# State space stages: TensorE takes u*B first and the sum one unit behind, the gate follows the second scan, ScalarE draws items a unit later

## The chip, the cores and the metric

One core of a Trainium2 chip runs the whole program. The metric is the time of one execution on the device, in microseconds. Engines are named as the profile names them: TensorE (PE, its weight loads PEld), VectorE (DVE), ScalarE (ACT), GpSimd (POOL) and SyncE (SP), which issues DMAs.

## The reference, cut to what matters

The model is a decoder of two layers on an activation x of 4 batches x 512 positions x 256 channels, all in float32. Each layer is a state space block (Mamba), a cross attention and a feed forward part. The change touches the two state space blocks only. For one batch such a block computes:

```
xz = h @ in_proj_w.T;  x, z = split(xz)              # 512 inner channels each
xc = silu(conv4(x) + conv_b)                          # causal, 4 taps per channel
dt, Bm, Cm = split(xc @ x_proj_w.T)                   # 16 states in Bm and in Cm
dt = softplus(dt @ dt_proj_w.T + dt_proj_b)
h[t] = exp(dt[t] * A) * h[t-1] + (dt*xc)[t] * Bm[t]   # for each channel and each of 16 states
y[t] = sum over states of h[t] * Cm[t]
out = ((y + D * xc) * silu(z)) @ out_proj_w.T         # then added to the residual
```

The recurrence over t is the large part: 4 batches x 512 channels x 16 states x 512 positions, in each of the two blocks.

## The kernel before, in words

The program runs seven stages one after the other, with a barrier between neighbours. Stages "A" (from about 40 to 580 us of the span) and "B" (from about 1620 to 2160 us) are the state space blocks; both are written by the same functions, `mamba_pe`, `mamba_act`, `mamba_dve`, `mamba_pool` and `mamba_sp`.

**Units.** A stage has 128 units, 32 for each batch. A section of 8 units treats 128 inner channels (one partition each), a unit treats 2 of the 16 states at 512 positions, so a unit is a tile of 128 x 1024. Below, n is the number of a unit within its batch (0 to 31) and g within its section (0 to 7). For unit i:

- ScalarE makes the decays exp(dt*A) (`mamba_decay_act`, L656, two activations), in its slot i-2, so that it runs two units ahead. For g = 0, 1, 2, 4 and 6 they go to one of three PSUM places, used in turn (`i % RING_A`), and wait until unit i-3 has left that place; for g = 3, 5, 7 they go to one of two SBUF places.
- The input u*B with u = dt*xc: GpSimd multiplies it for g = 0, 1, 2, 4, 6 (L389); for g = 3, 5, 7 TensorE makes it with 8 matmuls against diagonal matrices (`mamba_input_pe`, L405), issued in its slot i-2.
- VectorE runs the scan over the positions (L850), then multiplies by the rows of C (L872) for g = 0, 1, 4, 6. For g = 2, 3, 5, 7 GpSimd multiplies (L430).
- TensorE sums: 8 transposing matmuls against the identity add the unit to y in PSUM (L543). For g = 0 this is preceded by D*xc (L538), which has to wait until the gate of the section before has read y.
- After the eighth sum of a section VectorE gates: yzT = y * silu(z) (`mamba_gate_dve`, L769). Before the change it is issued behind the scan of g = 0 of the next section and ahead of that unit's multiply.
- The products (`ch`) lie in a ring of four; whoever writes unit i waits for the sum of unit i-4.

**Items.** The dense work of the neighbouring batches is spread over the units as items: `h` (rows turned, L118), `in` and `z` (the halves of in_proj, L479 and L482), `conv` (L506), `xp` (L510), `dt` (L514), `bt` and `ut` (turns of B and of u), `yt` (the gated y turned back) and `out` (out_proj, L519). The tables `OWN`, `BEFORE` and `AHEAD` give for each n which item of this batch, of the one before and of the one after is due, and `mamba_items(i)` lists them for a unit. All items share one PSUM bank: an item on TensorE first waits until the item before has been drawn. ScalarE draws all items but `out`, which VectorE draws by adding it to x (L791) behind scan i+1, and `bt`, which VectorE's diagonals (L781) draw.

**Order of work.** Each engine has one hand written list and works it off in order. Before the change, TensorE's slot i is: the items of i, the input u*B of i+2, the sum of i. ScalarE's slot i is: the decays of i+2, `conv` items of slot i-1, the other items of slot i, then the occasional long ones: rows for the next batch (n = 4), silu of z (n = 5), a square root (n = 14), silu of the convolution (n = 22), the softplus (n = 26 to 28). Silu, square root and logarithm each need another activation table than the decays' exponential: a table load ahead and one behind.

Of the kernel before, what the change touches and what calls it, by code (L numbers as in the profile page):

```python
# [17 lines left out]
B, T, D = 4, 512, 256  # L18
# [151 lines left out]
UNITS = 8  # L170
PER = 4 * UNITS
RING_A = 3
RING_C = 4
# [5 lines left out]
def mamba_make(k, ctx, L, R, rms, rnd):  # L179
# [47 lines left out]
    if rms:  # L227
# [21 lines left out]

FIRST = [("h", 0), ("h", 1)] + [("in", i) for i in range(4)] + [("conv", 3), ("xp", 0)] + [("dt", i) for i in range(4)] + [("bt", 0)]  # L250
FIRST_BANKS = (0, 1, 2, 3, 4, 5, 6, 7, 0, 1, 3, 6, 2)
OWN = {1: ("z", 0), 2: ("z", 1), 3: ("z", 2), 4: ("z", 3), 13: ("yt", 0), 18: ("yt", 1), 25: ("yt", 2)}
BEFORE = {1: ("yt", 3), 6: ("out", 0), 8: ("out", 1), 10: ("out", 2), 12: ("out", 3)}
AHEAD = {5: ("h", 0), 6: ("h", 1), 7: ("in", 0), 9: ("in", 1), 11: ("in", 2), 14: ("in", 3),
         15: ("conv", 0), 17: ("conv", 1), 19: ("conv", 2), 21: ("conv", 3),
         23: ("xp", 0), 24: ("dt", 0), 25: ("dt", 1), 26: ("dt", 2), 27: ("dt", 3), 30: ("bt", 0)}


def mamba_items(i):

    b, s = i // PER, i % PER
    o = []
    if i == 0:
        o.append(("ut", 0, 0))
    if b and s in BEFORE:
        o.append((BEFORE[s][0], b - 1, BEFORE[s][1]))
    if s in OWN:
        o.append((OWN[s][0], b, OWN[s][1]))
    if s % UNITS == 6 and i // UNITS + 1 < 4 * B:
        n = i // UNITS + 1  # L270
        o.append(("ut", n // 4, n % 4))
    if b + 1 < B and s in AHEAD:
        o.append((AHEAD[s][0], b + 1, AHEAD[s][1]))
    return o


# [16 lines left out]
def from_pe(i):  # L293

    return i % UNITS in FROM_PE
# [15 lines left out]
def mamba_out(m, i):  # L311

    return m.met(MET[i]) if by_pool(i) else m.out(i - MET[i])
# [206 lines left out]
    p.then_inc(*m.full.up)  # L520


def mamba_pe(k, m, pe):
    for w, j in FIRST:
        mamba_item_pe(k, m, pe, w, 0, j)
    pe.wait_ge(*m.drawn(LEAD - 1))
    for i in range(PER * B):
        s, g = i // UNITS, i % UNITS
        for item in mamba_items(i):
            mamba_item_pe(k, m, pe, *item)  # L530
        if i + 2 < PER * B and from_pe(i + 2):
            mamba_input_pe(k, m, pe, i + 2)
        if g == 0:
            if s:
                pe.wait_ge(*m.gated(s - 1))
            pe.wait_ge(*m.dx_in(s))
            for c in range(4):
                p = pe.matmul(m.y[:, c, :], m.dx[:, 128 * c:128 * c + 128], k.ident, start=c == 0, stop=False, is_transpose=True)  # L538
            p.then_inc(*m.direct.up)
        pe.wait_ge(*mamba_out(m, i))  # L540
        for j in range(2):
            for c in range(4):
                p = pe.matmul(m.y[:, c, :], m.ch[i % RING_C][:, j, 128 * c:128 * c + 128], k.ident, start=False,  # L543
                              stop=g == UNITS - 1 and j == 1 and c == 3, is_transpose=True)
        p.then_inc(*m.summed.up)
    mamba_item_pe(k, m, pe, "yt", B - 1, 3)
    for j in range(4):
        mamba_item_pe(k, m, pe, "out", B - 1, j)
# [111 lines left out]
def mamba_act(k, m, act):  # L660
# [32 lines left out]
    for i in range(PER * B):  # L693
        b, n = i // PER, i % PER
        if i + 2 < PER * B:
            mamba_decay_act(k, m, act, i + 2)

        for item in mamba_items(i - 1) if i else []:
            if item[0] == "conv":
                mamba_item_act(k, m, act, *item)  # L700
        for item in mamba_items(i):
            if item[0] != "conv":
                mamba_item_act(k, m, act, *item)
        if i == 1:
            for j in range(1, B):
                x_stats_act(k, act, 4 * m.rnd + j)
            if m.rms:
                act.activation(m.t0[:, 4:NT], k.xmv[:, 4:NT, 1], ACT.Sqrt).then_inc(*m.dev.up)
        if i in (8, 9):
            for j in range(8) if i == 8 else range(4):  # L710
                o, n0 = (m.dg, 4) if i == 8 else (m.dg0, 0)
                g = act.activation(o[:, j, :], k.ident, ACT.Identity, scale=cw[:, n0 + j:n0 + j + 1])
            g.then_inc(*m.diag.up)
        if n == 14 and b:
            x_stats_act(k, act, 4 * (m.rnd + 1) + b - 1)
        if n == 5:
            mamba_gate_act(k, m, act, b)
        if n == 4 and b + 1 < B:
            mamba_rows_act(k, m, act, b + 1)
        if n % UNITS == 3 and i // UNITS + 1 < 4 * B:  # L720
            mamba_direct_act(k, m, act, i // UNITS + 1)
        if n == 22 and b + 1 < B:
            mamba_silu_act(k, m, act, b + 1)
        if n in (26, 27) and b + 1 < B:
            mamba_soft_exp_act(k, m, act, b + 1, 2 * (n - 26), 2 * (n - 26) + 2)
        if n == 28 and b + 1 < B:
            mamba_soft_log_act(k, m, act, 3 * b + 5, 0, 4)
    mamba_item_act(k, m, act, "yt", B - 1, 3)
# [78 lines left out]
def mamba_dve(k, m, dve):  # L807
# [25 lines left out]
    for i in range(PER * B):  # L833
# [14 lines left out]
            dve.wait_ge(*m.fed(NTH[i]))  # L848
            decays, inputs = a, m.bu[NTH[i] % 2][:, :, :]
        dve.tensor_tensor_scan(flat(to), flat(decays), flat(inputs), 0.0, ALU.mult, ALU.add).then_inc(*m.scan.up)  # L850
        if g == 0 and s:
            mamba_gate_dve(k, m, dve, s - 1)
        if i == 4:
            for j in range(1, B):
# [3336 lines left out]
```

## Time and profile before

| | |
|---|---|
| median of 3 runs | 2939.02 us (2935.67 to 2941.57) |
| the profiled execution's own time | 2939.04 us |
| its span, first to last instruction | 2936.8 us |
| mean granted TensorE clock | 0.888 of full speed |
| PE busy / DVE / ACT / POOL, whole span | 83% / 70% / 55% / 36% |
| stage A, first to last scan | 51.7 to 572.2 us |
| stage B, first to last scan | 1633.0 to 2152.4 us |

How to read it: the span and the own time differ by 2.2 us, and both differ from the median by nothing that matters, so a difference taken from the trace can be added to the median. The two stages are a good third of the span. The shares of busy time are means over stages with different limits; inside a state space stage the scans have a fixed cadence, and what stretches the stage is seen between two scans.

### The profile page before, as it was taken

Reading aid. Unit: us, or ns where it says so; the run is one execution under the profiler, and the core shown is the slowest. Engines: PE = TensorE matmul, PEld = TensorE weight load, DVE = VectorE, ACT = ScalarE, POOL = GpSimd, SP = SyncE. Lnnn points to the kernel's source line nnn. Section 1 sums busy time; section 2 is a strip of 40 time slices with the busy share of each in tenths; the row PEclk is TensorE's granted clock in tenths of the full one; section 3 lists DMA queues with packets and bytes.
Section 4 is the critical chain, followed back from the end, with each engine's and each line's share of the span. In section 5 each row is a group of like instructions: output and inputs, shape, how many; then the busy total and the mean of one; then the engine's idle time right before and its main releaser. Section 6 shows DMA issues by size and latency. Waiting matters only on the chain.

```text
span 2936.8 us, 38603 instructions
## 1 busy us (share of the span) xinstructions
PE 2436.4 (83%) x14260; PEld 1906.8 (65%) x14260; DVE 2051.7 (70%) x3042; ACT 1606.3 (55%) x2716; POOL 1051.3 (36%) x777
## 2 busy tenths in 40 slices
PE   5878787668998799858995688787777897899998
PEld 3556566556776588757883456565653443789998
DVE  5767777779998466547885777776855654567776
ACT  6565655344665454535884765655612445357763
POOL 2766667600000154210211567766821235100004
PEclk8989898889999799978997798897986887889999
DMA  4020212093000000012421220202046331246653
GB/s 148 1 94 1 94 34 85 0 333 98 23 1 1 35 1 30 8 63 97 151 104 50 95 72 23 94 2 95 11 71 96 72 101 58 85 148 216 216 205 91
DMA packets 98173, 235.14 MB, mean 80 GB/s; under 512 B 8902, under 2 KB 64978, under 8 KB 90819
## 3 DMA queue, kind: packets, MB, share of 16 engines
q1 hardware_dynamic: 85074, 209.85, 22.2%
q0 software_dynamic: 5376, 14.70, 1.5%
q10 hardware_dynamic: 7536, 8.13, 1.0%
q8 instruction: 115, 1.88, 0.3%
q14 instruction: 72, 0.58, 0.1%
HBM read 175.38 MB, written 48.81 MB: 76 GB/s over the span
## 4 chain that ended last, share of the span: by engine, by line
PE 49%; DVE 21%; ACT 12%; issue 7%; POOL 7%; DMA 1%; SPq 1%; POOLq 1%; ACTq 0%; DVEq 0%
PE psum L111 7%; PE psum L113 6%; PE psum L112 6%; PE psum L543 5%; PE psum L118 4%; PE psum L405 3%; POOL ch L430 3%; DVE ch L850 3%; PE psum L506 2%; PE psum L482 2%; ACT g L3770 2%; PE psum L479 2%; DVE psum L850 2%; POOL bu L389 2%; DVE ch L872 2%
## 5 line engine op out<-in xcount | busy, mean ns | idle before, releaser
L389 POOL TENSOR_TENSOR bu<-u,row 128x1024 f32<-128x1024 f32 x158 | 371.5, 2358 | 264.7 <-DVE psum L850 177.2
L543 PE MATMUL psum<-ident,ch 128*128 128x128 f32 x2048 | 299.7, 296 | 114.5 <-POOL ch L430 97.0
L543 PEld LDWEIGHTS psum<-ident,ch 128*128 128x128 f32 x2048 | 255.8, 153 | 165.3 <-POOL ch L430 112.2
L430 POOL TENSOR_TENSOR ch<-ch,row 128x1024 f32<-128x1024 f32 x128 | 300.5, 2352 | 137.4 <-DVE ch L850 137.4
L850 DVE TENSOR_TENSOR_SCAN psum<-psum,bu 128x1024 f32<-128x1024 f32 x128 | 292.1, 2282 | 18.7 <-ACT psum L656 18.3
L850 DVE TENSOR_TENSOR_SCAN ch<-ad,psum 128x1024 f32<-128x1024 f32 x96 | 218.8, 2279 | 102.6 <-PE psum L405 85.0
L405 PEld LDWEIGHTS psum<-row,uT 128*128 128x128 f32 x1536 | 196.7, 204 | 36.8 <-issue 33.0
L656 ACT ACTIVATE psum<-dt,A 128x511 f32<-128x511 f32 x320 | 207.9, 683 | 0.3
L405 PE MATMUL psum<-row,uT 128*128 128x128 f32 x1536 | 201.5, 288 | 0.0
L3770 ACT ACTIVATE g<-psum,bias 128x256 f32<-128x256 f32 x248 | 101.3, 471 | 133.7 <-PE psum L113 129.6
L872 DVE TENSOR_TENSOR ch<-psum,row 128x1024 f32<-128x1024 f32 x128 | 156.4, 1222 | 3.1
L111 PE MATMUL psum<-WH,hs 128*128 128x256 f32 x496 | 144.9, 292 | 5.1 <-DVE hs L3850 2.2
L111 PE MATMUL psum<-xT,WH 128*128 128x256 f32 x496 | 142.0, 286 | 7.6 <-DVE xT L3813 7.6
L3592 POOL DMA_INDIRECT R<-m1res,gi x26 | 26.2, 1007 | 340.5 <-DMA m1res<-ob 324.3
L112 PE MATMUL psum<-xT,WH 128*128 128x256 f32 x496 | 141.3, 285 | 0.0
L113 PE MATMUL psum<-xT,WH 128*128 128x256 f32 x496 | 141.3, 285 | 0.0
L113 PE MATMUL psum<-WH,hs 128*128 128x256 f32 x496 | 140.6, 284 | 0.0
L112 PE MATMUL psum<-WH,hs 128*128 128x256 f32 x496 | 140.2, 283 | 0.0
L3850 DVE TENSOR_TENSOR hs<-g,hs 128x512 fp32r<-128x512 f32 x124 | 85.6, 693 | 73.4 <-ACT hs L3777 71.3
L3367 POOL TENSOR_SCALAR_AFFINE_SELECT pT<-pT 128x256 f32<-128x256 f32 x128 | 53.5, 423 | 227.9 <-ACT pT L3139 226.9
L3139 ACT ACTIVATE pT<-psum 128x1024 f32<-128x1024 f32 (+3 forms) x128 | 87.6, 706 | 75.6 <-PE psum L3049 74.8
L656 ACT ACTIVATE ad<-dt,A 128x511 f32<-128x511 f32 x192 | 127.2, 712 | 0.1
(469 smaller groups left out, 6965.4 us busy)
## 6 DMA issues: line engine op xcount, KB each, us to landing
W<-in_m1W SPq DMA_DIRECT2D x24, 2052.0 KB, 8.7
row<-Ascr SPq DMA_DIRECT2D x52, 512.0 KB, 4.9
row<-Bscr SPq DMA_DIRECT2D x52, 512.0 KB, 5.0
m1buf<-zt SPq DMA_DIRECT2D x8, 2048.0 KB, 16.7
W<-in_m0W SPq DMA_DIRECT2D x16, 1024.0 KB, 5.8
m1res<-ob ACTq DMA_DIRECT2D x23, 256.0 KB, 5.0
m0buf<-zt SPq DMA_DIRECT2D x2, 2064.0 KB, 17.9
xe<-m0buf SPq DMA_DIRECT2D x8, 516.0 KB, 8.3
```

Of the source, the lines that this page charges most:

```text
L111: pe.matmul(o, al, bh, start=start, stop=False)
L112: pe.matmul(o, ah, bl, start=False, stop=False)
L113: return pe.matmul(o, ah, bh, start=False, stop=stop)
L118: return pe.transpose(o, i, k.ident[0:n, 0:n])
L389: e.tensor_tensor(m.bu[n % 2][:, :, :], u, m.row[:, g, 0, :, :], ALU.mult).then_inc(*m.fed.up)
L405: p = pe.matmul(m.a[i % RING_A][:, j, 128 * c:128 * c + 128], m.uT[:, c, :], m.diag_B[g][:, j, c, :], start=True, stop=True)
L430: pool.tensor_tensor(o, o, m.row[:, i % UNITS, 1, :, :], ALU.mult).then_inc(*m.met.up)
L543: p = pe.matmul(m.y[:, c, :], m.ch[i % RING_C][:, j, 128 * c:128 * c + 128], k.ident, start=False, stop=g == UNITS - 1 and j == 1 and c == ...
L656: e = act.activation(a[:, j, 1:T], m.dt[:, s % SIX, 1:T], ACT.Exp, scale=m.A[:, n:n + 1])
L850: dve.tensor_tensor_scan(flat(to), flat(decays), flat(inputs), 0.0, ALU.mult, ALU.add).then_inc(*m.scan.up)
L872: dve.tensor_tensor(m.ch[i % RING_C][:, :, :], a, m.row[:, g, 1, :, :], ALU.mult).then_inc(*m.out.up)
L3770: e = act.activation(g[:, 256 * o:256 * o + 256], m.hb[j][:, 256 * o:256 * o + 256], ACT.Gelu_apprx_tanh, bias=m.bias[w % 3][:, 2 * j + o: ...
```

## The change

It reorders the lists; the arithmetic, the tiles and the number of instructions stay the same.

1. TensorE's slot i becomes: input u*B of i+2, then the sum of unit i-1 (with D*xc in front where that unit opens a section), then the items of i. The sum of the last unit stands behind the loop.
2. VectorE gates a section behind the scan of g = 1 of the next section instead of g = 0.
3. ScalarE draws all items of slot i-1 in its slot i; before, only `conv` was drawn a slot later.
4. Within a slot an item of the batch before comes last, and the tables move most items by a slot or two. `h` 0 moves from 5 to 6, `h` 1 from 6 to 7, where `out` 0 now follows it; `out` comes at 7, 9, 11, 13 instead of 6, 8, 10, 12; `yt` 0 moves from 13 to 15, ahead of `conv` 0.
5. silu of z moves from n = 5 to 6, silu of the convolution from 22 to 21, and the first exponential of the softplus from 26 to 25.

```diff
-OWN = {1: ("z", 0), 2: ("z", 1), 3: ("z", 2), 4: ("z", 3), 13: ("yt", 0), 18: ("yt", 1), 25: ("yt", 2)}
-BEFORE = {1: ("yt", 3), 6: ("out", 0), 8: ("out", 1), 10: ("out", 2), 12: ("out", 3)}
-AHEAD = {5: ("h", 0), 6: ("h", 1), 7: ("in", 0), 9: ("in", 1), 11: ("in", 2), 14: ("in", 3),
-         15: ("conv", 0), 17: ("conv", 1), 19: ("conv", 2), 21: ("conv", 3),
-         23: ("xp", 0), 24: ("dt", 0), 25: ("dt", 1), 26: ("dt", 2), 27: ("dt", 3), 30: ("bt", 0)}
+OWN = {2: ("z", 0), 3: ("z", 1), 4: ("z", 2), 5: ("z", 3), 15: ("yt", 0), 19: ("yt", 1), 27: ("yt", 2)}
+BEFORE = {1: ("yt", 3), 7: ("out", 0), 9: ("out", 1), 11: ("out", 2), 13: ("out", 3)}
+AHEAD = {6: ("h", 0), 7: ("h", 1), 8: ("in", 0), 10: ("in", 1), 12: ("in", 2), 14: ("in", 3),
+         15: ("conv", 0), 16: ("conv", 1), 18: ("conv", 2), 20: ("conv", 3),
+         22: ("xp", 0), 23: ("dt", 0), 24: ("dt", 1), 25: ("dt", 2), 26: ("dt", 3), 30: ("bt", 0)}
...
 def mamba_pe(k, m, pe):
...
     for i in range(PER * B):
-        s, g = i // UNITS, i % UNITS
+        if i + 2 < PER * B and from_pe(i + 2):
+            mamba_input_pe(k, m, pe, i + 2)
+        if i:
+            mamba_sum_pe(k, m, pe, i - 1)
         for item in mamba_items(i):
             mamba_item_pe(k, m, pe, *item)
-        if i + 2 < PER * B and from_pe(i + 2):
-            mamba_input_pe(k, m, pe, i + 2)
...
+    mamba_sum_pe(k, m, pe, PER * B - 1)
...
         for item in mamba_items(i - 1) if i else []:
-            if item[0] == "conv":
-                mamba_item_act(k, m, act, *item)
-        for item in mamba_items(i):
-            if item[0] != "conv":
-                mamba_item_act(k, m, act, *item)
+            mamba_item_act(k, m, act, *item)
...
-        if n == 5:
+        if n == 6:
             mamba_gate_act(k, m, act, b)
...
-        if n == 22 and b + 1 < B:
+        if n == 21 and b + 1 < B:
             mamba_silu_act(k, m, act, b + 1)
-        if n in (26, 27) and b + 1 < B:
-            mamba_soft_exp_act(k, m, act, b + 1, 2 * (n - 26), 2 * (n - 26) + 2)
+        if n in (25, 27) and b + 1 < B:
+            mamba_soft_exp_act(k, m, act, b + 1, n - 25, n - 23)
...
-        if g == 0 and s:
+        if g == 1 and s:
             mamba_gate_dve(k, m, dve, s - 1)
```

`mamba_sum_pe` is new and holds the former end of the slot unchanged: the wait for the gate and D*xc where g = 0, the wait for the product, the 8 matmuls.

## Rows read from the trace of the kernel before

**Rows 1.** Windows by batch: length, busy PE, PEld, DVE, ACT, POOL, then PEclk, DMA

```profile
51.65:96.43 44.78, 34.56 (x175) 25.48 (x176) 35.01 (x27) 36.28 (x62) 28.98 (x15) 0.82 0.11 43
96.43:186.39 89.96, 74.75 (x408) 51.83 (x406) 64.58 (x37) 57.14 (x102) 62.31 (x30) 0.89 0.22 71
186.39:234.92 48.53, 37.68 (x191) 27.76 (x192) 32.67 (x23) 23.43 (x40) 31.40 (x16) 0.81 0.04 11
234.92:320.58 85.66, 72.95 (x431) 53.05 (x429) 67.41 (x48) 59.32 (x101) 62.30 (x30) 0.96 0.23 75
320.58:368.91 48.33, 37.49 (x191) 27.48 (x192) 32.66 (x22) 23.42 (x40) 31.39 (x16) 0.82 0.03 11
368.91:456.99 88.08, 76.38 (x431) 54.73 (x429) 67.29 (x48) 59.20 (x101) 61.55 (x30) 0.94 0.21 72
456.99:501.62 44.63, 35.62 (x190) 27.97 (x191) 32.46 (x22) 19.85 (x33) 32.03 (x16) 0.77 0.16 54
501.62:569.96 68.34, 47.15 (x344) 43.39 (x342) 61.84 (x45) 33.30 (x62) 54.80 (x25) 0.90 0.00 1
1632.96:1766.83 133.87, 108.88 (x580) 76.61 (x580) 95.84 (x59) 93.05 (x162) 91.42 (x44) 0.87 0.17 63
1766.83:1903.02 136.19, 113.83 (x620) 83.02 (x620) 99.97 (x70) 82.67 (x141) 93.68 (x45) 0.89 0.15 51
1903.02:2039.07 136.05, 113.95 (x620) 82.89 (x620) 99.95 (x69) 82.65 (x141) 93.63 (x45) 0.89 0.15 51
2039.07:2150.12 111.05, 80.86 (x532) 69.58 (x532) 94.29 (x66) 52.95 (x95) 86.12 (x40) 0.87 0.04 12
```

**Rows 2.** Waits in 186.39 to 320.58: total us, times, longest

```profile
DVE yzT L769 <- PE psum L543: 16.3, 4, 5.6
DVE ch L850 <- PE psum L405: 9.0, 7, 2.4
```

**Rows 3.** Waits in 456.99 to 572.3, the last batch of stage A

```profile
DVE yzT L769 <- PE psum L543: 10.8, 4, 3.9
```

**Rows 4.** Groups by line in 186.39 to 320.58: count, busy us, mean ns, idle before

```profile
L430 POOL TENSOR_TENSOR ch<-ch,row 128x1024 f32<-128x1024 f32 x16 | 37.6, 2353 | 15.3 <-DVE ch L850 15.3
L850 DVE TENSOR_TENSOR_SCAN ch<-ad,psum 128x1024 f32<-128x1024 f32 x12 | 27.4, 2282 | 13.8 <-PE psum L405 9.0 <-ACT psum L656 2.4 <-ACT ad L656 2.4
L872 DVE TENSOR_TENSOR ch<-psum,row 128x1024 f32<-128x1024 f32 x16 | 19.5, 1222 | 0.4
L506 PE MATMUL psum<-xs,dg 128*128 128x512 f32 x32 | 14.5, 594 | 0.0
```

**Rows 5.** Timeline 215.9 to 225, and one row of 283 to 296

```profile
216.19 1.04 PE L543 MATMUL psum<-ident,ch 128*128 128x128 f32 x8
217.07 1.89 PE L519 MATMUL psum<-outw,yz 128*128 128x256 f32 x8
217.29 1.91 ACT L626 ACTIVATE sz<-sz 128x2048 f32<-128x2048 f32 x1
219.27 1.28 ACT L656 ACT_TABLE_LOAD   x1
220.56 1.30 ACT L656 ACTIVATE psum<-dt,A 128x511 f32<-128x511 f32 x2
221.80 0.57 ACT L587 COPY uT<-psum 128x512 f32<-128x512 f32 x1
222.43 1.12 PE L118 MATMUL psum<-ident,xn 128*128 128x128 f32 x4 [2.30 <-ACT uT L587]
...
286.13 2.19 ACT L621 ACTIVATE xc<-xc 128x512 f32<-128x512 f32 x4
```

**Rows 6.** Windows around two idle stretches of TensorE, columns as in rows 1

```profile
146.53:149.94 3.41, 0.78 (x8) 0.54 (x5) 3.21 (x2) 3.38 (x5) 3.41 (x3) 1.00 0.01 2
149.94:156.76 6.82, 6.05 (x8) 1.45 (x8) 0.00 (x0) 3.26 (x6) 2.34 (x2) 0.50 0.00 0
285.00:288.40 3.40, 0.07 (x1) 0.00 (x0) 2.50 (x2) 3.38 (x7) 3.40 (x3) 1.00 0.00 0
```

More of the change, by code:

```diff
@@ L264, in mamba_items @@
         o.append(("ut", 0, 0))
-    if b and s in BEFORE:
-        o.append((BEFORE[s][0], b - 1, BEFORE[s][1]))
     if s in OWN:
@@ L273, in mamba_items @@
         o.append((AHEAD[s][0], b + 1, AHEAD[s][1]))
+    if b and s in BEFORE:
+        o.append((BEFORE[s][0], b - 1, BEFORE[s][1]))
     return o
@@ L520, in mamba_item_pe, with mamba_sum_pe @@
     p.then_inc(*m.full.up)
+def mamba_sum_pe(k, m, pe, i):
+    s, g = i // UNITS, i % UNITS
+    if g == 0:
+        if s:
+            pe.wait_ge(*m.gated(s - 1))
+        pe.wait_ge(*m.dx_in(s))
+        for c in range(4):
+            p = pe.matmul(m.y[:, c, :], m.dx[:, 128 * c:128 * c + 128], k.ident, start=c == 0, stop=False, is_transpose=True)
+        p.then_inc(*m.direct.up)
+    pe.wait_ge(*mamba_out(m, i))
+    for j in range(2):
+        for c in range(4):
+            p = pe.matmul(m.y[:, c, :], m.ch[i % RING_C][:, j, 128 * c:128 * c + 128], k.ident, start=False,
+                          stop=g == UNITS - 1 and j == 1 and c == 3, is_transpose=True)
+    p.then_inc(*m.summed.up)
 def mamba_pe(k, m, pe):
@@ L527, in mamba_pe @@
     for i in range(PER * B):
-        s, g = i // UNITS, i % UNITS
+        if i + 2 < PER * B and from_pe(i + 2):
+            mamba_input_pe(k, m, pe, i + 2)
+        if i:
+            mamba_sum_pe(k, m, pe, i - 1)
         for item in mamba_items(i):
             mamba_item_pe(k, m, pe, *item)
-        if i + 2 < PER * B and from_pe(i + 2):
-            mamba_input_pe(k, m, pe, i + 2)
[L533 to L545, printed above, removed]
+    mamba_sum_pe(k, m, pe, PER * B - 1)
     mamba_item_pe(k, m, pe, "yt", B - 1, 3)
```

## The prediction

> **What bounds the kernel now.** I read the windows first, because the change touches only the two state space stages, and in them only the order in which the 32 units of a batch run. S0, S1, ... S31 are the starts of a unit's scan within its batch; S32 is S0 of the next. The windows run from S0 to S0, those of stage A in two pieces (S0 to S10, S10 to S32; the last one ends at S31); behind the length stand the busy times of PE, PEld, DVE, ACT and POOL, then the clock [rows 1]. The first three batches of stage A cost 134.7 us (44.78 + 89.96), 134.2 and 136.4, those of stage B 133.9, 136.2 and 136.1; the last, which has no batch behind it to prepare, 113.0 and 111.1 up to S31. In the second batch (186.39 to 320.58, 134.2 us) VectorE is busy 100.1 us (32.67 + 67.41), TensorE 110.6, GpSimd 93.7, ScalarE 82.8: no engine is the bound by its work; they hand work to each other and wait.
>
> The waits say where. In that batch VectorE stands 16.3 us before its 4 gates, until TensorE has the last sum of the section before, and 9.0 us before scans whose input TensorE makes (L405) [rows 2]. In the last batch the gates cost 10.8 us [rows 3]. TensorE and ScalarE in turn are tied by the one bank: an item starts when the one before is drawn. The timeline shows the worst knot [rows 5]: silu of z takes 1.91 us from 217.29, a table load 1.28 from 219.27, decays 1.30, and only at 221.80 does ScalarE draw `ut`; TensorE goes on at 222.43.
>
> **The change part by part.** I walk one middle batch, with times from S0. A scan is 2.28 us, a multiply 1.22, GpSimd's product 2.35 [rows 4]; issue overlaps a little, so I step 2.2 for a scan alone and 3.46 for one with its multiply. A sum is 1.04, `out` 1.89 [rows 5], and `in`, `z` and u*B I take like `out`; `conv` is 14.5 / 4 = 3.6, and so I take `xp` [rows 4]. A hand over is about 0.1 us (0.06 from 222.37, the end of the draw, to 222.43).
>
> (a) *Gate behind the second scan.* GpSimd's last product of a batch is done within 3 us of S0, its sum 1 to 2 us later; the gate stands at S0 + 6.9 now and waits for nothing. One diagonal stays before the multiply of unit 0: S1 at 4.6, S2 at 8.7 (3.46 + 0.6 for the gate), S3 at 10.9.
>
> (b) *u*B first.* The input of unit 3 can start with the multiply of unit 0 (4.7) and is ready at 6.6, or 8.6 at half clock, ahead of S3. Those of 5 and 7 stand ahead of a sum and a `z` in their slots and come at 16 and 23, within 1 us of their scans. S8 comes at 25.2. Some 5 of the 9.0 us before L405's scans go in this part.
>
> (c) *Sum behind, items last, drawn a slot later.* This gives it back. `z` 0 to `z` 3 take turns with ScalarE's decays and the rows of the next batch; the last is drawn at 26.2. Then the knot: two loads 2.6, silu 1.9, decays 1.3, `ut` 0.6 [rows 5]: `ut` is drawn at 32.6. Before, `h` 0 had run ahead of the knot and `out` 0 inside it; now `ut`, `h` 0, `h` 1 and `out` 0 (slots 6 and 7) go behind it in single file: `h` 0 0.6 and its draw 0.7, decays 1.4, draw of `h` 1 0.7, `out` 0 1.9: 38.0. VectorE adds `out` 0 between scan 8 and its multiply, so it stands from 27.6 to 38.0: 10 us, in place of the waits before scan 8 and the first gate. S9 at 39.5, sum 7 is done by then, S10 at 39.5 + 4.1 = 43.6. Half clock behind the pause adds 2.4 (half of `h` and `out` again), a slow start of the batch up to 2 more: 48. I take 45.5, the middle, against 48.53 and 48.33 [rows 1]: -2.9 a middle batch.
>
> (d) *S10 to S32.* `out` 2 and `out` 3 stand behind u*B and a sum and come 1.9 and 0.9 us after VectorE asks, S14 at 56.5. The `ut` of slot 14 is drawn in slot 15 now, behind the square root and its two loads: at 66.4 instead of S14 + 4. `in` 3 ends at 68.3, `yt` 0 at 69.7, is drawn behind decays 18 at 71.0, `conv` 0 (now in slot 15) ends at 74.7 and the sum of unit 15, behind it, at 75.5. The second gate could start at 70.9: it waits 4.7. `conv` 1 and then `conv` 2 stand ahead of the inputs of 19 and 21: S19 at 80.9, S21 at 88.3. Silu of the convolution (2.19 [rows 5] and two loads) is ahead of decays 24 now, which come at 100.7, 2.9 us late. `ut` is drawn behind decays 25, `xp` ends at 106.3, `dt` 0 and sum 23 at 108.9: the third gate waits 2.4. S31 waits for the decays behind the softplus (127.3), S32 for `bt`: 133.7, at full clock. That is 90.1 from S10, against 85.66 and 88.08 [rows 1]. Bounds: 86, if the new order costs nothing here; 100, if half clock meets each knot. I take 92: the walk and 2 us of half clock, since such stretches are few in that piece before (clock 0.96 and 0.94 [rows 1]).
>
> (e) *First batch.* No `out`, no `yt` 3: `h` 1 ends at 33 and the first gate waits 1 us. Stage A keeps a chain of small VectorE operations at unit 4. I take -3.8 (A) and -6.9 (B) up to S10, and -2 each behind it, where the same knots stand. Bounds for the two batches: -26 and 0.
>
> (f) *Last batch.* `out` 0 still waits for silu: -2.6 (A) and -1.8 (B) up to S10. Behind it the gates other than the first have all of 10.8 less some 4.6 to give [rows 3], 1 us comes back at `out` 2 and 3: -5 each. Bounds for the two: -22 and -6.
>
> (g) *At nothing.* The number of instructions stays. The moved exponentials of the softplus use the decays' table and lie beside `dt` on TensorE. The last sum has its place. SyncE's loads of the next rows follow `xp`, drawn at 106.9 here and at 106.3 before, with 15 us in hand before input 32; if that cover went, S32 would be later by the excess. D*xc is a slot later and is covered by the ring of four.
>
> Sum. Stage A: first -5.8; two middle, (45.5 + 92) against a mean of 135.3, +2.2 each; last -7.6: -9.0. Stage B: first -8.9; two middle, 137.5 against 136.1, +2.8 in all; last -6.8: -12.9. Together -22. The profiled execution took 2939.04 us (span 2936.8, 2.2 us around it unchanged), the median is 2939.02: 2917.
>
> **The clock.** One stretch in which TensorE did little (146.53 to 149.94, 0.78 us of work) is followed by one at half clock, 1.2 GHz, in which 8 matmuls of `xp` took 6.05 us; another (285.00 to 288.40, 0.07 us of work) kept its clock [rows 6]. So a pause is paid for in some cases only. My walk has three pauses of 5 to 6 us in a middle batch, before `h` 0, `in` 3 and `xp`, where before they were shorter. The Trainium skill ("TensorE: Matmul & The Clock Gate", Part 1) says that the throttled clock is the default and that only activity releases it; by that rule the longer pauses would nearly always be paid for, and the time would be R3's, below. The trace agrees in one of the two stretches.
>
> **The rivals.** *R1, VectorE is freed.* The gates' waits go and nothing takes their place: all of them would be 6 x 16.3 + 2 x 10.8 = 119 us [rows 2, 3]; half, 60, gives 2880. For it: the gates are the largest wait, and a scan and a multiply more (3.5 us) cover most of one (5.6 at the longest). Against it: `out` 0 stands before the multiply of unit 8.
>
> *R2, nothing moves.* The turns that TensorE and ScalarE take over the one bank set the pace of three batches in four, whatever stands around them; in my walk `in` 1 to `dt` 3 come within 3 us of where they were. Middle batches then cost 3 us more than I count and the first ones gain 6 less: 2917 + 12 + 6 = 2935.
>
> *R3, slower.* One mechanism: the pauses behind silu of z, the square root and silu of the convolution bring half clock in every batch, and the work behind them (`h` and `out` 0; `in` 3 and `conv` 0; `xp`) is what VectorE waits for. Price 2.4 + 4 + 3.2 = 9.6 us (each of these lengths once more, less what decays hide), of which some 3 are counted; over four middle batches 27, and 5 in the first ones: 2949. From 5 us a middle batch more than I count it makes the kernel slower.
>
> **How the numbers follow.** Forecast 0.42, R1 0.15, R2 0.18, R3 0.25. A measurement can't tell less than 0.2% (5.9 us) from no change: 2933.1 to 2944.9. Faster: 0.36 from the forecast, 0.15 from R1, 0.06 from R2, 0.57. Same: 0.04, 0.12 from R2 and 0.03 from R3, 0.19. Slower: 0.02 from the forecast and 0.22 from R3, 0.24. The range starts at 2890, where the better bounds of (d), (e) and (f) lie in part, and ends at 2953, past R3; most of R1 and what lies above R3 are outside.
>
> **What would show it.** The gates' wait falls from 16.3 us a middle batch to about 7, that before L405's scans from 9 to about 3. New is VectorE's wait for `out` (L791 on L519), 10 us at unit 8 and 1 to 2 at 12 and 14, and one for decays at unit 24. S10 comes at 45 rather than 48, the last batch is 7 us shorter. I am wrong if L791 waits under 5 us a middle batch, if middle batches take under 130 or over 143 us, or if anything outside the two stages moves.

## The result, and the profile after

The changed kernel runs in 2928.34 us (median of 7 runs), the kernel before in 2941.57 (median of 7). By the medians it is 13.2 us faster, where 22 were forecast; the ratio is 0.9954, 95% interval 0.9939 to 0.9969. One of the seven runs of the changed kernel took 7603.46 us and is left out of the ratio. The profiled execution has a span of 2922.8 us against 2936.8.

The windows by batch, cut at the same units as those of before (columns as there: length, PE, PEld, DVE, ACT, POOL, clock, DMA):

```profile
51.57:93.50 41.93, 29.19 (x154) 23.49 (x155) 35.07 (x26) 34.48 (x59) 30.20 (x15) 0.77 0.11 45
93.50:179.22 85.72, 72.98 (x428) 51.86 (x426) 64.59 (x37) 59.70 (x106) 62.34 (x30) 0.93 0.22 75
179.22:222.26 43.04, 33.75 (x193) 27.29 (x194) 31.62 (x21) 22.63 (x38) 30.29 (x15) 0.83 0.03 13
222.26:318.10 95.84, 78.01 (x429) 55.86 (x427) 67.54 (x50) 60.30 (x102) 63.32 (x31) 0.90 0.20 67
318.10:363.43 45.33, 36.04 (x193) 29.02 (x194) 31.70 (x21) 22.64 (x38) 30.30 (x15) 0.79 0.03 12
363.43:459.00 95.57, 78.34 (x429) 55.33 (x427) 67.42 (x49) 60.42 (x102) 63.29 (x31) 0.90 0.20 67
459.00:499.44 40.44, 31.57 (x181) 25.71 (x182) 31.62 (x22) 18.87 (x31) 30.34 (x15) 0.82 0.17 56
499.44:563.20 63.76, 48.08 (x353) 43.89 (x351) 62.17 (x46) 33.38 (x62) 54.56 (x25) 0.92 0.00 1
1622.41:1749.42 127.01, 101.56 (x580) 74.80 (x580) 96.15 (x58) 93.80 (x163) 92.55 (x45) 0.88 0.20 73
1749.42:1888.17 138.75, 111.73 (x620) 82.95 (x620) 99.15 (x69) 82.73 (x140) 93.65 (x45) 0.88 0.15 50
1888.17:2029.07 140.90, 114.48 (x620) 84.29 (x620) 99.13 (x69) 82.81 (x140) 93.59 (x45) 0.86 0.14 50
2029.07:2133.28 104.21, 79.73 (x532) 69.62 (x532) 93.79 (x67) 52.24 (x93) 84.90 (x39) 0.88 0.04 13
```

Read against [rows 1]: the first batches are 7.1 and 6.9 us shorter, the last ones 8.8 and 6.8, and each of the four middle batches is longer, by 4.7, 4.5, 2.6 and 4.9. In a middle batch the first ten units are 1.6 to 5.5 us shorter, the 22 behind them 6.5 to 10.2 us longer. From first to last scan the two stages fall from 1040.0 us (520.6 + 519.4) to 1027.1 (513.9 + 513.1), by 13.0; all else changes by 1.1.

The waits of the second batch of stage A, for [rows 2] (us in total, times, longest):

```profile
DVE X L794 <- PE psum L519: 14.6, 3, 11.4
DVE yzT L772 <- PE psum L536: 10.7, 2, 6.4
DVE ch L853 <- PE psum L405: 5.9, 4, 1.7
```

The gates' wait has shrunk from 16.3 us to 10.7 and that for L405 from 9.0 to 5.9. First stands a wait that was 0.7 us in the kernel before: VectorE has to add `out` before it may go on. The row of before, in its second batch:

```profile
DVE X L791 <- PE psum L519: 0.7, 3, 0.2
```

In the last batch the gates wait 0.5 instead of 10.8 us [rows 3], `out` takes 9.6:

```profile
DVE X L794 <- PE psum L519: 9.6, 3, 8.8
DVE yzT L772 <- PE psum L536: 0.5, 1, 0.5
```

Single operations last what they lasted [rows 4] (the forms apart, 179.22 to 318.10), but `xp`, 8 matmuls of 593 ns before in this batch, took 793 each; the last row is that of the kernel before:

```profile
L430 POOL TENSOR_TENSOR ch<-ch,row 128x1024 f32<-128x1024 f32 x17 | 40.0, 2354 | 27.8 <-DVE ch L853 27.8
L853 DVE TENSOR_TENSOR_SCAN ch<-ad,psum 128x1024 f32<-128x1024 f32 x12 | 27.3, 2279 | 9.8 <-PE psum L405 5.9 <-ACT ad L663 2.8 <-ACT psum L663 1.1
L875 DVE TENSOR_TENSOR ch<-psum,row 128x1024 f32<-128x1024 f32 x16 | 19.5, 1220 | 0.3
L506 PE MATMUL psum<-xs,dg 128*128 128x512 f32 x32 | 14.7, 601 | 1.1 <-ACT yz L596 1.1
L510 PE MATMUL psum<-xc,xpw 128*48 128x512 f32 x8 | 5.1, 793 | 4.8 <-ACT uT L594 4.8
...
L510 PE MATMUL psum<-xc,xpw 128*48 128x512 f32 x8 | 3.6, 593 | 3.4 <-ACT xc L621 3.4
```

The timeline of the knot at silu of z, the counterpart of [rows 5], and behind the dots the one at the square root (start, length, engine and line, in brackets the idle time before):

```profile
203.25 2.27 DVE L853 TENSOR_TENSOR_SCAN psum<-psum,bu 128x1024 f32<-128x1024 f32 x1
205.26 1.91 ACT L633 ACTIVATE sz<-sz 128x2048 f32<-128x2048 f32 x1
209.77 0.57 ACT L594 COPY uT<-psum 128x512 f32<-128x512 f32 x1
210.40 1.11 PE L118 MATMUL psum<-ident,xn 128*128 128x128 f32 x4 [5.74 <-ACT uT L594]
214.11 0.69 ACT L566 ACTIVATE hT<-psum,PV 128x512 f32<-128x512 f32 x1 [0.59 <-PE psum L118]
214.85 2.00 PE L519 MATMUL psum<-outw,yz 128*128 128x256 f32 x8 [0.78 <-ACT hT L566]
216.88 0.42 DVE L794 TENSOR_TENSOR X<-X,psum 128x256 f32<-128x256 f32 x1 [11.36 <-PE psum L519]
...
241.83 0.30 ACT L148 ACTIVATE xsd<-xmv,t 128x4 f32<-128x4 f32 x1 [3.75 <-DVE xmv L135]
245.35 3.60 PE L479 MATMUL psum<-hT,inw 128*128 128x512 f32 x4 [5.55 <-ACT uT L594]
251.44 3.70 PE L506 MATMUL psum<-xs,dg 128*128 128x512 f32 x8 [1.15 <-ACT yz L596]
256.05 0.69 DVE L772 TENSOR_TENSOR yzT<-psum,sz 128x512 f32<-128x512 f32 x1 [6.43 <-PE psum L536]
```

TensorE stands idle for 5.74 us until ScalarE has drawn `ut` (209.77 to 210.34). `h` 0, `h` 1 and `out` 0 follow in single file, and VectorE, done with its scan at 205.5, waits 11.36 us. At n = 14 the same happens behind the square root: `in` 3 starts after 5.55 us of idleness, at half clock (3.60 us), and `conv` 0 (3.70) goes ahead of the sum for which the gate waits 6.43. This knot is more than two table loads: the root itself waits 3.75 us for VectorE's statistics of x (L135), since it now stands ahead of the draws of slot 14. In the kernel before it stood behind these draws and waited for nothing (activation at 256.28, right behind its load).

### The profile page after: what moved, and what is told of

Its sections match the earlier page's. It is cut to its first block, busy times and chain, and to the rows that moved or that the text cites. A ratio compares the mean times of both kernels' runs of the same rounds, so it can differ in the third digit from the quotient of the medians.

```text
span 2922.8 us, 38603 instructions
## 1 busy us (share of the span) xinstructions
PE 2419.1 (83%) x14260; PEld 1907.1 (65%) x14260; DVE 2048.1 (70%) x3042; ACT 1606.6 (55%) x2716; POOL 1051.6 (36%) x777
## 4 chain that ended last, share of the span: by engine, by line
PE 51%; DVE 18%; ACT 18%; issue 7%; POOL 2%; DMA 1%; SPq 1%; ACTq 1%; POOLq 1%; DVEq 0%
PE psum L111 6%; PE psum L112 6%; PE psum L113 6%; PE psum L405 4%; PE psum L536 4%; PE psum L118 4%; PE psum L506 3%; ACT WH L3626 3%; PE psum L519 2%; ACT g L3773 2%; ACT psum L663 2%; PE psum L482 2%; PE psum L479 2%; PE psum L3067 1%; DVE psum L853 1%
## 5 line engine op out<-in xcount | busy, mean ns | idle before, releaser
L536 PE MATMUL psum<-ident,ch 128*128 128x128 f32 x2048 | 288.5, 290 | 43.8 <-POOL ch L430 42.8
L853 DVE TENSOR_TENSOR_SCAN psum<-psum,bu 128x1024 f32<-128x1024 f32 x128 | 291.7, 2279 | 19.6 <-ACT psum L663 19.5
L405 PEld LDWEIGHTS psum<-row,uT 128*128 128x128 f32 x1536 | 202.5, 209 | 59.2 <-issue 40.1
L405 PE MATMUL psum<-row,uT 128*128 128x128 f32 x1536 | 209.5, 295 | 20.7 <-ACT uT L594 13.7
```

The lines of the kernel that those rows point to most:

```text
L405: p = pe.matmul(m.a[i % RING_A][:, j, 128 * c:128 * c + 128], m.uT[:, c, :], m.diag_B[g][:, j, c, :], start=True, stop=True)
```

## The experiments

All lengths are those of the two stages together, first to last scan, read from the traces. The kernel of E5 was traced twice and gave 982.7 and 983.3; every other kernel was traced once, that of before too. Batches of one trace with the same list differ more: by up to 2.2 us in before, 4.3 in E4, 8.0 in E12. So a difference of a few us between two rows of the table shows nothing. The rest of the kernel, which no experiment touches, is between 1893 and 1915 us long in the fourteen traces, so a single total time can't tell 20 us. "Stages" in the table below is the length of the two stages together.

| run | kernel | stages, us | against before |
|---|---|---|---|
| | before | 1040.0 | |
| | changed | 1027.1 | -13.0 |
| E1 | before + later gate | 1010.5 | -29.5 |
| E2 | before + TensorE's order | 1054.4 | +14.4 |
| E3 | changed, gate back | 1090.7 | +50.7 |
| E4 | changed, draws back in their slot | 1006.2 | -33.8 |
| E5 | before + later gate + order | 982.7 | -57.3 |
| E6 | changed, silu at 7, out 0 before h 1 | 1002.4 | -37.6 |
| E7 | E4, out 0 before h 1 | 993.9 | -46.1 |
| E8 | changed, square root at 15 | 1027.3 | -12.7 |
| E9 | changed, conv behind sum and input | 1046.6 | +6.5 |
| E10 | E5 again, timed | 983.3 | -56.7 |
| E11 | E7 with E9's places for conv | 997.3 | -42.8 |
| E12 | E5 with draws a slot later | 1029.1 | -10.9 |

My theory after the result: the later gate is what gains; the later draws and the new places of the items make knots at which TensorE waits for ScalarE and VectorE for TensorE. Its rival: the change is worth its sum of parts, and the item chain over one bank holds everything else.

**E1, the gate alone.** On the kernel before:

```diff
-        if g == 0 and s:
+        if g == 1 and s:
             mamba_gate_dve(k, m, dve, s - 1)
```

> The kernel before with one line changed: VectorE gates a section behind the scan of g = 1. Theory (each wait before a gate shrinks by at most the 3.46 us of one scan and multiply, and part comes back before scans that wait for TensorE's u*B, which still stands behind the sum that waits for the gate): middle batches 134 to 136 us become 129 to 132, the two stages together 25 us shorter than the kernel before. Rival A (the gate was the bound): 10 us or more a batch, 80 us together. Rival B (TensorE's list sets the pace, the gate's place is worth nothing without the new list): under 5 us together.

Stages 1010.5 us, 29.5 shorter, near the theory's 25; middle batches 133.0 to 133.2. The waits of its second batch:

```profile
DVE ch L850 <- PE psum L405: 15.6, 8, 5.2
DVE yzT L769 <- PE psum L543: 1.2, 1, 1.2
```

The gates' 16.3 us have shrunk to 1.2, but the scans fed by L405 now wait 15.6 instead of 9.0. This one line is worth more than the whole change.

**E2, TensorE's order alone.** `mamba_pe` and `mamba_sum_pe` from the changed kernel, all else from before.

> The kernel before with TensorE's slot alone in the new order: u*B of i+2, sum of i-1, items of i. Gate, tables and ScalarE's draws as before. Theory: the 9 us a middle batch before scans that wait for L405 fall under 3, the wait before the gate grows because the sum of a section's last unit now stands in the next slot behind u*B and the items of its own; together 10 to 25 us shorter than before. Rival A: the order brings nothing without the later gate, 0 or longer, since the gate's wait grows by what L405 gives. Rival B: this part carries the whole gain of the changed kernel in first and last batches (7 us each).

Stages 1054.4 us, 14.4 longer. The wait for L405 falls to 1.2 us in the second batch, the gates' grows to 22.6:

```profile
DVE yzT L776 <- PE psum L536: 22.6, 4, 12.8
DVE ch L857 <- PE psum L405: 1.2, 1, 1.2
```

Rival A holds: with the gate behind the first scan the order costs more than it gives.

**E3, the changed kernel with the gate back.**

```diff
-        if g == 1 and s:
+        if g == 0 and s:
             mamba_gate_dve(k, m, dve, s - 1)
```

> The changed kernel with the gate back behind the scan of g = 0. Theory: at the batch's start the gate costs 3.5 us again, behind units 8 and 16 it is hidden by the waits for out 0 and for the sum behind conv 0; so 4 to 6 us a batch, 30 to 45 us together longer than the changed kernel, most of it seen in the last batch (gates 2 and 3). Rival: the later gate is worth nothing in the new order, under 10 us together.

Stages 1090.7 us, 63.7 longer than the changed kernel, where I had expected 30 to 45. All four gates wait, 34.7 us in the second batch with 14.5 for the longest, since `out` 0 and `conv` 0 stand ahead of the sums they need. I had thought the second and third of them hidden behind other waits.

**E4, the draws back in their own slot.**

```diff
         for item in mamba_items(i - 1) if i else []:
+            if item[0] == "conv":
+                mamba_item_act(k, m, act, *item)
+        for item in mamba_items(i):
+            if item[0] != "conv":
                 mamba_item_act(k, m, act, *item)
```

> The changed kernel with ScalarE's draws back in their own slot (conv a slot later, as before the change). Theory (the later draw lengthens the knots at silu of z and at the square root): ut and h 0 are drawn ahead of silu, ut and in 3 of slot 14 ahead of the square root, so the wait of VectorE for out 0 falls from 11.4 us to 7 or 8 and the second gate's from 6.4 to 3; together 30 us shorter than the changed kernel. Rival (drawn in its own slot, ScalarE stands waiting for TensorE's items and the decays come late): scans wait for decays (L663), and the stages are 10 us or more longer than in the changed kernel.

Stages 1006.2 us, 20.8 shorter than the changed kernel. In the second batch the gates wait 4.3 us instead of 10.7 and the wait for `out` is 13.2 instead of 14.6; its longest fell from 11.4 to 10.0, where I had expected 7 or 8; of the rival the waits for decays come true (12.8 us instead of 6.6) without turning the balance.

**E5, gate and order on the old tables.** E1 and E2 together.

> The kernel before with two of the parts: the gate behind the scan of g = 1 and TensorE's slot in the new order; tables and draws as before. Gate alone made the two stages 29.5 us shorter, order alone 14.4 longer. Theory (the order only takes the wait before scans fed by L405, 15.6 us a middle batch under the gate alone, and its price was the gate's wait, which the later gate hides): the two stages are 40 to 60 us shorter than before, middle batches 127 to 131. Rival A (the parts add up, 29.5 - 14.4): 10 to 20 us shorter. Rival B (the wait moves from L405 to ScalarE's decays, which the turns over the one bank delay): as the gate alone, 25 to 35 us shorter, with the wait for decays over 18 us a middle batch.

Stages 982.7 us, 57.3 shorter than before, as the theory has it; rival B's wait for decays comes too, but without its price. The parts don't add up (-29.5 and +14.4 would make -15): each takes away a wait that the other one creates (E1 left 15.6 us before L405's scans, E2 22.6 before the gates). The waits of its second batch:

```profile
DVE psum L857 <- ACT psum L663: 19.8, 7, 6.7
DVE X L798 <- PE psum L519: 4.0, 4, 1.6
DVE yzT L776 <- PE psum L536: 2.2, 2, 1.5
DVE ch L857 <- PE psum L405: 0.7, 1, 0.7
```

Gates and L405 are done with (2.2 and 0.7 us); what is left is ScalarE's decays (19.8, and 2.8 more in another row), late, as far as the waits tell, because it stands waiting for items: in this batch 12.8 us for `yt`, 12.8 for `in` and 8.7 for `conv`. No run took these waits away.

**E6, out 0 ahead of h 1.** Silu of z moves to n = 7, and in slot 7 the item of the batch before comes first:

```diff
-        if n == 6:
+        if n == 7:
             mamba_gate_act(k, m, act, b)
...
+    if b and s == 7:
+        o.append((BEFORE[s][0], b - 1, BEFORE[s][1]))
     if b + 1 < B and s in AHEAD:
         o.append((AHEAD[s][0], b + 1, AHEAD[s][1]))
-    if b and s in BEFORE:
+    if b and s in BEFORE and s != 7:
```

> The changed kernel with silu of z a slot later (n = 7 instead of 6) and out 0 ahead of h 1 in slot 7. Theory (out 0 behind silu of z and h 1 is what VectorE waits 11.4 us for at unit 8): that wait falls to 3 to 5 us, S10 of a middle batch comes 5 to 8 us earlier, at 36 to 39 instead of 43 to 45, the last batch gains 4 to 6; the two stages together 35 to 50 us shorter than in the changed kernel. Rival (in 0 to dt 3 keep their times, since silu now stands before h 1 is drawn, so what is won at unit 8 is lost again by the gate of unit 17): 10 us or less together.

Unit 10 of a middle batch starts at 35.3 to 35.5 us instead of 43 to 45, as expected; the middle batches are only 2.6 to 4.4 us shorter than in the changed kernel (136.2 to 136.5), the stages 24.6, of which the two last batches give 12.7. The wait for `out` moved from unit 8 (3.7 us now) to unit 10 (5.3), and the gate of unit 17 waits 7.0. The truth lies between theory and rival.

**E7, the same on E4**, where silu stays at n = 6.

> The kernel of the fourth experiment (the changed one, each item but conv drawn in its own slot) with out 0 ahead of h 1 in slot 7. There h 0 is drawn 10 us before out 0 ends, since silu and two table loads stand between. Theory: out 0 follows h 0 at once, VectorE's wait for out at unit 8 falls from 10 us to under 2, S10 of a middle batch at 35 instead of 43.5; together 30 to 45 us shorter than the fourth, that is 60 to 80 shorter than before. Rival (the next wait is for the draw of in 0 and the gate, which h 1 behind silu delays): 10 to 20 shorter than the fourth.

Stages 993.9 us, 12.3 shorter than E4: the size is the rival's. Of its mechanism only a part shows: a new wait of 2.9 us for `out` stands behind unit 10, but the gates wait 4.3 us as in E4. Unit 10 of a middle batch starts at 37.3 to 38.1 instead of 43.1 to 43.6, and the waits for decays grow (15.4 us instead of 12.8).

**E8, the square root a slot later.**

```diff
-        if n == 14 and b:
+        if n == 15 and b:
             x_stats_act(k, act, 4 * (m.rnd + 1) + b - 1)
```

> The changed kernel with the square root of n = 14 in slot 15, behind the draws of ut and in 3. Theory (ut waits 5.5 us for the square root's two table loads, and in 3, conv 0 and sum 15 with it): the second gate's wait falls from 6.4 us by 3 to 6 in the four middle batches, S18 comes that much earlier, 12 to 22 us together; the last batches, in which that gate does not wait, stay. Rival (decays 18, behind the later square root, or the half clock take its place): under 5 us together.

Stages 1027.3 us, as the changed kernel (1027.1): the theory missed, the rival holds. The gates of the second batch wait 13.1 us instead of 10.7, with 7.8 for the longest. `ut` is drawn 3.1 us earlier in the batch, but the root's two table loads now stand before the draw of `yt` 0, which is drawn as late as before (71.3 us into the batch; 71.6 in the changed kernel). `conv` 0 starts behind that draw after 4.13 us of idleness and takes 5.40 us instead of 3.70, part of it at half clock, and the sum of unit 15 is behind it. That makes the gate's wait 1.4 us longer.

**E9, the convolutions behind sum and input.**

```diff
-         15: ("conv", 0), 16: ("conv", 1), 18: ("conv", 2), 20: ("conv", 3),
-         22: ("xp", 0), 23: ("dt", 0), 24: ("dt", 1), 25: ("dt", 2), 26: ("dt", 3), 30: ("bt", 0)}
+         16: ("conv", 0), 17: ("conv", 1), 19: ("conv", 2), 21: ("conv", 3),
+         23: ("xp", 0), 24: ("dt", 0), 25: ("dt", 1), 26: ("dt", 2), 27: ("dt", 3), 30: ("bt", 0)}
...
-        if n == 21 and b + 1 < B:
+        if n == 22 and b + 1 < B:
             mamba_silu_act(k, m, act, b + 1)
-        if n in (25, 27) and b + 1 < B:
-            mamba_soft_exp_act(k, m, act, b + 1, n - 25, n - 23)
+        if n in (26, 28) and b + 1 < B:
+            mamba_soft_exp_act(k, m, act, b + 1, n - 26, n - 24)
```

> The changed kernel with conv 0 to 3 in slots 16, 17, 19, 21 instead of 15, 16, 18, 20, so that each stands behind the sum and the input that VectorE waits for; xp, dt, silu of the convolution and the first softplus exponential a slot later with them. Theory (conv 0 ahead of the sum of unit 15 makes the gate of unit 17 wait 6.4 us, in first batches 3.8; the convolutions ahead of u*B give 1.4 to 1.7 each at units 19, 21, 23): the gate's wait at unit 17 falls under 1.5, S18 comes 5 to 7 us earlier; together 20 to 35 us shorter than the changed kernel. Rival (the chain of items over the one bank is the pace, so xp and dt come as late as before and the wait turns up at units 24 to 31): 8 us or less together.

The step from unit 17 to 18 in the second batch falls from 10.45 us to 5.52, as the theory says, and the stages are 19.5 us *longer* (1046.6). The waits of its second batch:

```profile
DVE X L794 <- PE psum L519: 14.4, 3, 11.2
DVE ch L853 <- PE psum L405: 7.8, 4, 2.6
DVE yzT L772 <- PE psum L536: 6.9, 2, 5.4
DVE ch L853 <- ACT ad L663: 5.8, 1, 5.8
DVE psum L853 <- ACT psum L663: 5.4, 1, 5.4
```

The gates give 3.8 us; two waits for decays take back 5.7, 5.4 us before unit 25 and 5.8 before unit 31 (in the changed kernel 2.7 before unit 24 and 2.8 before unit 31), and L405 another 1.9. The cause as I read it, not tested by itself: silu of the convolution, `xp`, `dt` and the softplus all came a slot later. Here the chain of items is the pace, as the rival has it. The early convolutions, which I had counted as a loss, pay.

**E10, E5 timed.**

> The kernel of the fifth experiment timed: before, the gate behind the second scan and TensorE's new order, without the new tables and the later draws. Theory: its two stages are 57 us shorter than before in the trace, so the ratio to before is 0.980 to 0.982 against 0.9954 for the changed kernel. Rival (the other stages give part of it back, since their length differs from run to run by 10 to 20 us): 0.984 to 0.988.

2890.87 us against 2933.63 for before on the same chip, ratio 0.9845, interval 0.9815 to 0.9874. The trace has 983.3 us for the stages. The total falls by 43 us and not by 57, so the rival's size came, though the interval reaches to the theory's 0.980 to 0.982; the rival's reason is not shown. The traced execution of E10 is 50.3 us shorter than that of before, with 56.7 in the stages and 6.3 lost in the rest. Most of the remainder comes from the kernel before, whose eleven runs here lie between 2926.86 and 2948.80 us, while the six of E10 lie within 6.2. The kernel before was traced once, so whether its stages or its rest vary is open.

**E11, the repairs together.** E7 with the places of E9; the softplus exponentials stand at n = 26 and 27 as in the kernel before.

> All repairs on the changed kernel's tables: draws in their own slot, out 0 ahead of h 1, conv, xp and dt as in the ninth experiment. Theory (the knots found add up: draws 21 us, out 0 12 us, conv ahead of the sum 10 to 20 us): the two stages 45 to 60 us shorter than in the changed kernel, about level with the tenth (983 us for both), ratio 0.979 to 0.983. Rival (waits for decays take over once gates and out no longer wait, as in the fifth, where they are 22 us a middle batch): 990 us or more, ratio 0.984 or more.

2892.94 us, ratio 0.9851, interval 0.9822 to 0.9880; stages 997.3 us, 3.3 longer than E7. In the second batch waits for decays are 21.3 us (15.4 in E7), those of the gates 1.5, those for `out` 7.9 as in E7. The rival holds: what the gates no longer wait is waited for decays. Its stages are 14 us longer than E10's and its total only 2.1, so the rest is shorter by 10 in its trace (1893 against 1903): a gain in the stages is not the same gain in the total, for a reason that no run shows.

**E12, the draws a slot later on the old tables.** E5 with the changed kernel's loop over `mamba_items(i - 1)` and the softplus exponentials at n = 26 and 28.

> The kernel of the fifth experiment (tables of before, gate behind the second scan, new order on TensorE; both stages 983 us) with every item drawn a slot later, and the second softplus exponential at n = 28 for that. It fills the last place of the square of old or new tables and draws in the same slot or later (983; new and same 1006; new and later 1027). Theory (the later draw costs by itself, since every item then also waits for the next unit's decays): 15 to 30 us longer, 998 to 1013. Rival (the later draw costs only with the new tables, where ut, h 0, h 1 and out 0 are behind silu of z; with the old ones it takes away part of the 22 us a middle batch of waits for decays): 975 to 988.

Stages 1029.1 us, 46.4 longer than E5, half as much again as the 30 that I had at most expected. The waits of its second batch, one of 145.6 us (the other middle ones are 137.6, 140.0 and 145.6):

```profile
DVE yzT L772 <- PE psum L536: 13.3, 3, 6.0
DVE X L794 <- PE psum L519: 11.4, 4, 7.8
DVE ch L853 <- PE psum L405: 8.7, 4, 4.0
```

All three waits for TensorE that E5 had made short (2.2, 4.0, 0.7) are back. With it the square is full:

| stages, us (gate and order new) | drawn in own slot | drawn a slot later |
|---|---|---|
| old tables | 982.7 (E5) | 1029.1 (E12) |
| new tables | 1006.2 (E4) | 1027.1 (changed) |

So the later draws cost 46.4 us on the old tables and 20.8 on the new; the new tables cost 23.5 without them and nothing with them (2.1 us is less than equal batches of E12 differ). Gate and order gave 57.3 us, the two other parts took 44.4 back. Where in a batch they took it is shown in part only: `out` 0 behind silu of z is one place (E6, E7), while the square root and the convolutions, moved one at a time, gave no gain (E8, E9).

## Why the prediction was right, and where it was not

Time and sign were right: -22 forecast, -13.2 measured, 2928 us in a range of 2890 to 2953 that also held no change and a slower kernel. Term by term:

| term | forecast | measured |
|---|---|---|
| (a) to (c), S0 to S10 of a middle batch | 45.5 | 43.0, 45.3, 42.9, 45.3 |
| (d), S10 to S32 of a middle batch | 92 | 95.8, 95.6, 95.8, 95.6 |
| (e), first batches, both | -14.7 | -14.0 |
| (f), last batches, both | -14.4 | -15.6 |
| four middle batches | +7.2 | +16.6 |

The last three lines of the measured column sum to -13.0, the difference of the stages; the forecast for them was -21.9. The middle batches are 9.4 us worse than forecast, the others together 0.5 better. Stage B is cut at S10 like stage A.

**(a), the gate.** Right in its first step: S1 and S2 came 4.45 and 8.37 us into the batch, where 4.6 and 8.7 stood. I did not see what this part is worth by itself; E1 and E3 put it at 29.5 us on the old lists and 63.7 on the new.

**(b), u*B first.** Of the 5 us less before L405's scans came 3.1 (9.0 to 5.9); the last part of the prediction even had "about 3" left. That it gains only together with (a) was not in the text; E2 and E5 show it: +14.4 alone, 27.9 shorter (1010.5 to 982.7) on top of the later gate.

**(c), the knot at silu of z.** Right in mechanism and nearly in size: a wait for `out` at unit 8, forecast 10 us, measured 11.36 with half clock on `h`. `out` at units 12 and 14, forecast 1.9 and 0.9, measured 2.2 and 1.0. S10 came at 43.0 and 45.3 for two reasons that nearly cancel. `ut` was drawn 31.1 us into the batch and not at 32.6. From there to the end of `out` 0 it took 6.5 us in the second batch, where the walk had 5.4 at full clock, and 8.3 in the third, where `out` 0 too ran at half clock (3.77 us instead of 2.00) and VectorE waited 13.31. So half clock cost 1.1 and 2.9, where (c) named 2.4 and took a part of it. That 45.5 fits is in part luck. E6 confirms the place.

**(d), the mis-sized term.** The walk had S19 at 80.9, the decays of unit 24 at 100.7, S31 at 127.3 and S32 at 133.7; the trace of the second batch has S19 at 82.3, S24 at 102.2, S31 at 132.8 and S32 at 138.9. So the walk was 1.5 us short up to S24 and 5 at the end. The pauses are those of the walk (5.55 us before `in` 3, 4.80 before `xp`), but I counted 2 us for half clock and the rows show about 5 in that batch: `in` 3 took 3.60 instead of 1.9, `xp` 5.07 instead of 3.6, and one u*B (292.81 to 296.44) 3.63 instead of 1.95. It held up unit 27 by 1.09 us and `dt` 2 behind it, and so the softplus and the decays for which unit 31 waits. That is 1.7 + 1.5 + 1.7 = 4.9 where 2 were counted, so 2.9 of the 3.8 us over the forecast; the other 0.9 I can't place. The wait for decays at unit 24 was 2.7, where the walk had 2.9. So R3's mechanism was at work: with (c) half clock cost 6.0 us in the second batch and about 7 in the third (`in` 3 took 3.78 and `xp` 5.87 there, the u*B 2.05), where R3 named 9.6 and I counted some 3. But the u*B of the second batch was not in R3's list, and no pause stands ahead of it; its rows are in the last section.

**(e), (f).** Within 1.2 us each, by sums whose parts were further off: the first ten units of stage B's first batch gained 4.4 us instead of 6.9, the 22 behind them in stage A's 4.2 instead of 2. The gates' wait in the last batch fell from 10.8 to 0.5, and `out` waits 9.6 there.

**(g), at nothing.** Outside the stages the two traces differ by 1.1 us. That it is so little is luck: the rest differs by up to 22 us over the fourteen traces, and by 4 between the two of E5's kernel.

**The gates' wait.** Forecast 7 us a middle batch, measured 10.7 (6.4 and 4.3 instead of 4.7 and 2.4), which is about what `in` 3 and `xp` lost at half clock (1.7 and 1.5).

**R1** (gates go, nothing in their place, 2880) did not come for this kernel, but gate and order alone come near it: 57.3 us in the stages (E5), 43 in the total (E10), where R1 had 60. I held `out` 0 against it, and rightly: (c) had seen that slots and later draws put it behind silu. What the prediction had no term for is what these two parts cost in all, 44.4 us. **R2** came in part: the middle batches cost 2.3 us each more than forecast, where it had 3, while the first ones gained as forecast, and E9 fits its picture of the pace. It moved a convolution out of the way of a gate and lost 19.5 us at the end of the chain.

**What stays open.** Why E5's decays come late was read from its waits only (ScalarE busy with or waiting for items); no run took that wait away. The moved exponentials of the softplus and silu of the convolution were never changed alone. How much of the 44.4 us is half clock was not separated: the granted clock over both stages is 0.91 in E5 and 0.87 to 0.88 in the changed kernel, and 0.88 in before, so cause and effect go together.

## What to carry to other kernels

When several engines hand work around a ring, test the parts of a reordering one by one and in pairs. Here one line was worth 29.5 us, a second part cost 14.4 alone and gave 27.9 with the first, and the rest took 44.4 back; the whole, at 13, hid all of it. Parts moved alone in the tables then gave anything from -25 to +20 us.

A consumer that draws a shared buffer "one slot later" can lengthen each hand over by whatever stands first in the next slot; here it cost 20.8 us with one set of places and 46.4 with the other. Look in the timeline for long operations of the drawing engine (here table loads, silu, and a square root that waits for its input) and count how many items go behind them in single file.

Before moving an item out of the way of a wait, ask what chain the item belongs to and whether that chain ends on time: E9 repaired the visible wait and lost at the other end.

## What the runs showed of the hardware

TensorE's clock has two levels, 2.4 GHz and half of it, 1.2. In the second batch of the changed kernel each of its three long pauses (5.74, 5.55 and 4.80 us) was followed by half clock. The columns are those of the windows above, for a pause, the work behind it, a second pause, its work, a third pause and its work:

```profile
205.50:210.30 4.80, 0.00 (x0) 0.00 (x0) 0.02 (x1) 4.78 (x6) 4.22 (x2) 0.73 0.00 0
210.30:214.50 4.20, 3.67 (x16) 3.27 (x16) 0.00 (x0) 2.41 (x6) 0.00 (x0) 0.50 0.00 0
239.90:245.30 5.40, 0.00 (x0) 0.00 (x0) 5.40 (x11) 3.45 (x6) 3.70 (x3) 0.68 0.00 0
245.35:248.64 3.29, 3.29 (x4) 1.41 (x5) 3.26 (x3) 0.00 (x0) 3.29 (x2) 0.50 0.00 0
278.50:283.20 4.70, 0.00 (x0) 0.00 (x0) 1.99 (x2) 4.68 (x9) 2.34 (x1) 0.95 0.02 3
283.20:286.20 3.00, 2.94 (x4) 0.84 (x5) 2.97 (x3) 0.01 (x1) 2.35 (x1) 0.50 0.00 0
```

The clock falls within the pause in all three (0.73, 0.68 and 0.95 on average); in the third it falls at the end, and `xp` runs 3 us at half clock behind it. By the rule of the Trainium skill ("TensorE: Matmul & The Clock Gate", Part 1), that the throttled clock is the default and activity releases it, all three would be paid for, and the trace agrees. In [rows 6] it did not: one pause of 3.4 us was free.

A pause is not the only thing that the clock falls behind. The half clock of the u*B in (d) came behind a stretch in which TensorE was busy for 4.07 of 4.40 us, at full clock:

```profile
288.40:292.80 4.40, 4.07 (x20) 2.16 (x19) 1.34 (x2) 4.20 (x8) 1.20 (x1) 1.00 0.28 101
292.80:296.50 3.70, 3.70 (x19) 3.69 (x19) 2.68 (x2) 3.67 (x7) 0.94 (x1) 0.54 1.00 348
```

Why it fell there no run shows; the same u*B of the third batch took 2.05 us. Nor does the same pause always cost the same: behind 5.74 us before `h` 0, `out` 0 took 2.00 us in the second batch and 3.77 in the third.

The four activations of a middle batch that need another table (silu twice, the square root, the logarithm) cost a load of 1.28 us ahead and one behind, in every kernel here. Silu of z starts 0.02 us after its load, and the load 0.02 us after the copy before it. The Trainium skill ("ScalarE: Activation LUTs", What ACT_TABLE_LOAD costs) states about 1.28 us for the load as well, but about 1.38 more for a drain, for which these traces have no room.

A load does not wait for the input of the activation that it serves: the square root's load ran from 236.80 to 238.08 us, its activation came at 241.83 after 3.75 us of waiting for VectorE's statistics. So a wait for an input covers the load ahead of it.
